# Regrouping the weighted sums of a cross-attention pipeline: four groups a batch, four buffers of exponentials, and new slot tables

## The reference

```
x = layernorm(x + self_attention(x))
x = layernorm(x + cross_attention(x, ctx))   # 16 heads of 8; keys and values are ctx @ Wk + bk, ctx @ Wv + bv
x = layernorm(x + experts(x))                # 8 experts, the best 2 per token, capacity-limited
```

## Time and profile before

| | us |
|---|---|
| median of three runs | 974.03 |
| the profiled execution, device time | 974.64 |
| its span, first to last instruction | 972.5 |
| PE busy | 924.9 (95%) |
| DVE busy | 699.5 (72%) |
| ACT busy | 645.9 (66%) |
| POOL busy | 351.0 (36%) |

### The profile page before, as it was taken

How to read it: one execution, slowest core, us unless ns; L and a number is a source line. 1 busy time by engine, 2 the same in 40 slices (tenths; PEclk the granted TensorE clock), 3 DMA queues, 4 the chain that set the end, 5 groups by cost and what they waited for, 6 DMA issues and landing times.

```text
span 972.5 us, 28783 instructions
## 1 busy us (share of the span) xinstructions
PE 924.9 (95%) x10471; PEld 741.4 (76%) x10471; DVE 699.5 (72%) x1490; ACT 645.9 (66%) x1081; POOL 351.0 (36%) x332
## 2 busy tenths in 40 slices
PE   6777999999999999999999999999999999999995
PEld 4655777777777777777777777777777778999894
DVE  6673777767676677676767767767788857777996
ACT  4654777777777777777777777777776545445554
POOL 6452362222333333222233333332222413112992
PEclk8897999999999999999999999999999999999998
DMA  5538566666655555666666555566665201002321
GB/s 141 121 79 191 120 133 140 143 136 137 137 128 119 119 119 126 141 137 138 136 137 134 119 119 119 120 137 143 137 138 111 69 1 44 23 23 86 128 114 41
DMA packets 43626, 111.44 MB, mean 115 GB/s; under 512 B 15491, under 2 KB 26053, under 8 KB 43461
## 3 DMA queue, kind: packets, MB, share of 16 engines
q1 hardware_dynamic: 43572, 110.77, 50.3%
HBM read 32.23 MB, written 1.89 MB: 35 GB/s over the span
## 4 chain that ended last, share of the span: by engine, by line
PE 84%; ACT 5%; DVE 4%; issue 3%; SPq 2%; POOL 1%; DMA 1%; ACTq 0%; DVEq 0%; POOLq 0%
PE psum L1592 17%; PE psum L1424 16%; PE psum L1652 13%; PE psum L1431 8%; PE psum L1436 8%; PE psum L1656 4%; ACT arena L759 3%; PE psum L1679 2%; PE psum L1692 2%; PE psum L1691 2%; PE psum L1680 2%; PE psum L1681 2%; PE psum L1693 2%; PE psum L1441 1%; SPq L396 1%
## 5 line engine op out<-in xcount | busy, mean ns | idle before, releaser
L946 DVE TENSOR_REDUCE arena<-psum 128x1 f32<-128x500 f32 x672 | 447.8, 674 | 210.1 <-PE psum L1424 206.9
L759 ACT ACTIVATE arena<-psum 125x896 f32<-125x896 f32 x384 | 347.5, 916 | 109.0 <-PE psum L1592 101.7
L1424 PE MATMUL psum<-K_hi,Q_bd 128*128 128x500 f32 x672 | 319.6, 485 | 7.0 <-DVE arena L946 4.1
L547 POOL TENSOR_TENSOR arena<-arena,K_hi 128x500 fp32r<-128x500 f32 x96 | 120.7, 1257 | 403.3 <-ACT K_hi L690 403.3
L1592 PEld LDWEIGHTS psum<-Q_st,K_st 97*125 97x125 f32 x1536 | 221.6, 189 | 42.4 <-ACT arena L759 16.6
L1592 PE MATMUL psum<-Q_st,K_st 97*125 97x224 f32 x1536 | 238.6, 278 | 6.1 <-ACT arena L759 5.6
L1652 PE MATMUL psum<-arena 125*25 125x168 f32 x3072 | 170.5, 311 | 0.2
L1424 PEld LDWEIGHTS psum<-K_hi,Q_bd 128*128 128x128 f32 x672 | 128.6, 192 | 53.3 <-issue 20.8
L813 ACT ACTIVATE K_st<-psum 128x448 fp32r<-128x448 f32 x128 | 69.8, 545 | 79.5 <-PE psum L1681 78.0
L1656 PE MATMUL psum<-arena 125*9 125x56 f32 x3072 | 117.6, 213 | 0.0
L1656 PEld LDWEIGHTS psum<-arena 125*9 125x9 f32 x3072 | 94.1, 91 | 16.6
(11 more groups left out here) (249 smaller groups left out, 983.3 us busy)
## 6 DMA issues: line engine op xcount, KB each, us to landing
K_st<-K_hi SPq DMA_DIRECT2D x256, 187.5 KB, 4.8
K_st<-arena SPq DMA_DIRECT2D x128, 187.5 KB, 3.4
arena<-in_ctx SPq DMA_DIRECT2D x32, 562.5 KB, 6.8
arena<-gate_rows SPq DMA_DIRECT2D x8, 896.0 KB, 4.4
arena<-in_L_ffn_W SPq DMA_DIRECT2D x16, 256.0 KB, 3.2
Q_st<-max_row SPq DMA_DIRECT2D x224, 0.5 KB, 1.7
arena<-OS_all SPq DMA_DIRECT2D x12, 168.0 KB, 4.0
x_rows<-x_all SPq DMA_DIRECT2D x1, 896.0 KB, 6.4
```

Of the source, the lines that this page charges most:

```text
L547: g.tensor_tensor(low.bitcast(F32R), low, K_hi[:, par, n * KB:n * KB + KB].bitcast(F32), ALU.subtract).then_inc(F["keys_low"], 1)
L759: a.activation(P2[c % NP].rearrange("p (n k) -> p n k", n=2), psum[0:CK, 2 + 2 * (c % 2):4 + 2 * (c % 2), 0:HQ // 2], ACT.Exp)\
L946: v.reduce_max(mx[:, n // NB, n % NB:n % NB + 1], bank_of(n)[:, 0:KB], AX.X).then_inc(F["piece_max_taken"], 1)
L1424: mm(bank_of(n)[:, 0:KB], Q_bd[:, par].rearrange("p h q -> p (h q)")[:, 128 * (n // NB):128 * (n // NB) + 128], K_hi[:, par, (n % NB) * KB ...
```

## The change

It changes the order and the groups of the same arithmetic. No matmul, copy or DMA is added to a batch or taken from it.

- The weighted sums of a period stand in four groups of 3, 3, 2 and 4 chunks (slots 3, 6, 9, 11) instead of five of 2, 3, 3, 1 and 3 (slots 2, 5, 8, 10, 11).
- There are four buffers of exponentials instead of three (`NP`), so that an exponential waits for the sums of the chunk four before it.
- Six max pieces of a batch are taken in the period before the one that ends its maxima, instead of nine (`NEXT`). T stands in slot 9 instead of 8, behind V and ahead of O, and two pieces of the next batch come before it instead of one (`BEFORE_TURN`). The array `mx` is held twice.
- The slots of V, K, their copies, the steps on the sums and the scaling move.

```diff
-V_SLOTS = (9, 11, 3)
-K_SLOTS = (5, 6, 8)
-SUM_SLOT, TURN_SLOT = 0, 8
-V_COPIES = (9, 11, 3)
-K_COPIES = (4, 6, 7)
-EARLY_PIECES = {0: (9,), 1: (10,), 2: (11,), 3: (12,), 4: (14,), 6: (18,), 7: (20,), 9: (2,), 10: (4,), 11: (6,)}
-MID_PIECES = {3: (13,), 5: (15, 16), 6: (19,), 8: (0,), 9: (3,), 11: (7,)}
-LATE_PIECES = {5: (17,), 8: (1,), 10: (5,), 11: (8,)}
-OUTPUTS = {2: (0, 1), 5: (2, 3, 4), 8: (5, 6, 7), 10: (8,), 11: (9, 10, 11)}
-NP = 3
+V_SLOTS = (6, 9, 1)
+K_SLOTS = (3, 4, 7)
+COPY_SLOT, SUM_SLOTS, SCALE_SLOT = 0, (0, 1, 2, 2), 3
+ROW_SLOT, TURN_SLOT, KEEP_SLOT = 8, 9, 11
+V_COPIES = (5, 9, 1)
+K_COPIES = (2, 4, 7)
+NEXT, BEFORE_TURN = 6, 2
+EARLY_PIECES = {1: (6, 7), 3: (9, 10), 4: (11, 12), 6: (15,), 7: (19,), 9: (1,), 10: (3,)}
+MID_PIECES = {1: (8,), 6: (16, 17), 11: (4,)}
+LATE_PIECES = {4: (13,), 5: (14,), 6: (18,), 7: (20, 0), 9: (2,), 11: (5,)}
+OUTPUTS = {3: ((0, 0), (0, 1), (0, 2)), 6: ((0, 3), (0, 4), (0, 5)), 9: ((0, 6), (0, 7)), 11: ((0, 8), (0, 9), (0, 10), (0, 11))}
+NP = 4
...
         def bank_of(n):
-            return bank[0 if n == 0 else (n + 1) % 2]
+            return bank[(n + (n >= BEFORE_TURN) + 1 + BEFORE_TURN) % 2]
...
-            row_max(0)
+            row_max(0, 0)
+            for n in range(BEFORE_TURN - 1):
+                piece_max(1, 1, n)
             row_out(0)
...
-                if n == 2:
+                if n == BEFORE_TURN + 1:
                     if turns:
                         pe.wait_ge(F["max_row_ready"], b + PRIME)
...
-            def turn(b):
+            def turn(b, more):
 
                 pe.wait_ge(F["row_max_taken"], b + 1 + PRIME)
+                if more and BEFORE_TURN > 1:
+                    pe.wait_ge(F["piece_max_taken"], (b + 1) * PIECES + BEFORE_TURN - 1 + PRIME)
                 mm(bank[1][0:RG, 0:128], m2x, ident[:], start=True, stop=True).then_inc(F["max_transposed"], 1)
...
-            pieces1(0)
-            turn(0)
-            pieces1(1)
+            pieces1(*range(BEFORE_TURN))
+            turn(0, True)
+            pieces1(BEFORE_TURN)
```

More of the change, by code:

```diff
@@ L75 @@
 PLAIN = 9000.0
[L76 removed]
+ARENA = 19884
 PRIME = 4
@@ L192, in decoder_kernel @@
         inverse = at(128, SLOTS * S // 32)
-        mx = at(128, RG, NB)
+        mx = at(128, 2, RG, NB)
         used[0] = max(used[0], after1)
         K_lo = at(128, NK)
+        yT = [whole[:, used[0] + QC * i:used[0] + QC * i + QC] for i in range(2)]
         ctxT2 = at(DC + 1, 2, NK)
@@ L329, in pieces @@
         def pieces(c, table):
-            return [(2 if n < 9 else 1, n) for n in table.get(c, ())]
+            return [(2 if n < NEXT else 1, n) for n in table.get(c, ())]
         def bank_of(n):
-            return bank[0 if n == 0 else (n + 1) % 2]
+            return bank[(n + (n >= BEFORE_TURN) + 1 + BEFORE_TURN) % 2]
         def has(b, ahead):
@@ L749, in period @@
                 for c in range(NC):
-                    if c == 0 and has(b, -1):
+                    if c == COPY_SLOT and has(b, -1):
                         act.wait_ge(F["outputs_made"], b * NC + PRIME)
@@ L760, in period @@
                          .then_inc(F["weights_ready"], 1)
-                    if c == 9 and has(b, 1):
+                    if c == KEEP_SLOT and has(b, 1):
                         keep_extremes(b + 1)
@@ L939, in _, with piece_max, row_max @@
             dve.wait_ge(consts, 1)
-            def piece_max(b, n):
+            def piece_max(b, par, n):
                 dve.wait_ge(F["max_scores_made"], b * PIECES + n + 1 + PRIME)
[L944 to L948, removed]
+                if n == 0 and (not isinstance(b, int) or b >= 2):
+                    dve.wait_ge(F["row_max_taken"], b - 1 + PRIME)
+                v.reduce_max(mx[:, par, n // NB, n % NB:n % NB + 1], bank_of(n)[:, 0:KB], AX.X).then_inc(F["piece_max_taken"], 1)
+            def row_max(b, par):
                 dve.wait_ge(F["piece_max_taken"], (b + 1) * PIECES + PRIME)
@@ L988, in _, with taken @@
             v.memset(bank[6], 0.0).then_inc(F["bank_cleared"], 1)
[L989 to L992 removed]
+            for n in range(BEFORE_TURN + 2, NEXT):
+                piece_max(1, 1, n)
+            def taken(b, par, c, table):
                 for ahead, n in pieces(c, table):
@@ L995, in taken @@
                         continue
-                    piece_max(b + ahead, n)
+                    piece_max(b + ahead, (par + ahead) % 2, n)
             def period(b, par, half):
                 for c in range(NC):
[L1000 to L1003, removed]
+                    taken(b, par, c, EARLY_PIECES)
+                    taken(b, par, c, MID_PIECES)
+                    if c == ROW_SLOT and has(b, 1):
+                        row_max(b + 1, 1 - par)
                     if c == TURN_SLOT and has(b, 1):
@@ L1023, in period @@
                             v.transpose(R_sb, sums_T).then_inc(F["inverses_turned"], 1)
-                    if c == 4 and has(b, -1):
+                    if c == SCALE_SLOT and has(b, -1):
                         dve.wait_ge(F["inverses_turned"], b + PRIME)
@@ L1534, in _, with bank_free @@
             last.then_inc(w_ps, 1)
-            pieces1(2, 3)
+            pieces1(*range(BEFORE_TURN + 1, BEFORE_TURN + 3))
             pe.wait_ge(F["keys_copied"], 2 * NB + PRIME)
             value_project(1, 0)
-            pieces1(4, 5, 6, 7)
+            pieces1(*range(BEFORE_TURN + 3, NEXT - 1))
             pe.wait_ge(F["values_copied"], NB + 1 + PRIME)
             value_project(1, 1)
-            pieces1(8)
+            pieces1(NEXT - 1)
+            def bank_free(b, kind, n):
+                if isinstance(b, int) and b == B - 2:
+                    pe.wait_ge(F["keys_copied"], B * NB + PRIME)
+                    pe.wait_ge(F["values_copied"], B * NB - 1 + PRIME)
+                    return
+                i = [p[1:] for p in PROJECTIONS].index((kind, n))
+                if isinstance(b, int) and b == 0 and i == 0:
+                    pe.wait_ge(F["values_copied"], NB + 2 + PRIME)
+                _, last, m = PROJECTIONS[i - 1]
+                batch = 1 if last == "values" and m == 2 else 2
+                pe.wait_ge(F[f"{last}_copied"], b * NB + ((batch - (i == 0)) * NB + m + 1) + PRIME)
             def max_scores(b, par, c, table):
@@ L1624, in period @@
                         n = V_SLOTS.index(c)
[L1625 to L1628, removed]
+                        bank_free(b, "values", n)
                         value_project((par + ahead) % 2, n)
@@ L1639, in period @@
                     if c == TURN_SLOT and has(b, 1):
-                        turn(b + 1)
-                    if has(b, 0):
-                        for k in OUTPUTS.get(c, ()):
+                        turn(b + 1, has(b, 2))
+                    for ago, k in OUTPUTS.get(c, ()):
+                        if has(b, -ago):
                             if k == 0:
-                                if isinstance(b, int) and b == 0:
+                                if isinstance(b, int) and b - ago == 0:
                                     pe.wait_ge(F["bank_cleared"], 1 + PRIME)
[L1646 to L1650, removed]
+                                pe.wait_ge(F["values_copied"], (b + (1 - ago)) * NB + PRIME)
+                                if not isinstance(b, int) or b - ago >= 1:
+                                    pe.wait_ge(F["outputs_copied"], b - ago + PRIME)
+                            pe.wait_ge(F["weights_ready"], b * NC + (k + 1 - ago * NC) + PRIME)
+                            weights_, values = P2[k % NP], V2[(par + ago) % 2]
                             for m in range(4):
```

28 lines of the change are left out of this document (13 added, 15 removed).

## The result

The changed kernel takes 1037.64 us (median of four runs, 1034.92 to 1040.92) against 974.5 us for the kernel before beside it: 1.065 of its time, 95% interval 1.061 to 1.069. The forecast was 1000 us, 988 to 1010. The sign was right and the mechanism it named is in the trace; the size was short by 38 us, and the larger part of that belongs to a rival that had been given 3%.

What follows compares the result with a forecast made beforehand. It took PE to bound the kernel before and the row of maxima to bind after the change: 17 + 4.5 + 2.5 + 2 - 0.5 = +25.5 us on 974.0, rounded to 1000 us, range 988 to 1010.

Steps and rivals of the forecast that it cites:

- PE's work: PE in one steady loop period: 22.16 us less 0.33 for a group and 0.44 for a stall, 21.39 us.
- The stall at S of slot 2: PE waiting at S of slot 2 for the exponential of chunk 0: its 0.44 us a period would go.
- the gain of one group: One group of sums fewer on PE in each period: 0.33 us less.
- T's place: T, counted from S of slot 0: starts 16.4 us in, against 13.42 before, with 5.0 us of PE work behind it.
- The row's way: From T through row_out, seven DMA issues and landing: 6.2 us, making a wait of some 1.35 us each period.
- The clock: PE's granted clock in the loop: waits would not lower it, nothing added to the sum.
- rival C: PE's clock in the loop: a wait in every period drops it, 3 to 4.5 us each, 1090 to 1135 us; 3%.
- The start: Up to S of batch 1: later T and row_out(0) and a key copy moved to slot 2, +4.5 us.
- The end: Period of batch 30: DVE's output statistics and a projection stand before row_out and T, +2 us (0 to 3.5).
- A: Loop: the row does not bind, PE's work alone sets the period, some 955 us; 6%.
- B: Loop: the row binds but T comes at 15.8 us, period stays 22.16 us, 974 to 978 us; 3%.
- D: `K_lo` DMAs land over 1.1 us later than reckoned, S of slot 5 waits; at 0.5 a period, 1015 us; 6%.

Runs made afterwards that it cites:

- matmuls in the wait: Changed kernel with its seven DMAs, plus six matmuls of 448 columns ahead of PE's wait for the row in each period: 1014.19 us, 1.042 of before.
- one spare DMA: Changed kernel with one small DMA more ahead of the row's load in the periods of batches 1 to 28: 1062.33 us.
- the kernel with one DMA: Changed kernel with the row of maxima loaded by one DMA a period instead of seven: 957.98 us, 0.984 of before.
- six spare DMAs: Kernel before with six small DMAs issued by SP ahead of the row's load in the periods of batches 1 to 28: 1047.78 us, 1.077 of before.

## Why the prediction was right or wrong

**PE's work.** Right: 21.39 us forecast, 21.31 to 21.45 measured once the row was out of the way. The prices of the groups and the stall, read from the chain, were good to 0.1 us over a period, and K, O and V, T, O without an M between cost about what entries from M cost. The stall at S of slot 2 is gone: in the loop the list of waits has S waiting for no exponential. But what the prediction called the gain of one group is not a gain of the group by itself, as the groups alone gave nothing in the kernel before.

**T's place.** 16.4 us forecast, 16.55 measured; the 0.1 taken off was not there (the sum without it was 16.47). **The row's way** from T: 6.2 to the landing forecast, 0.52 + 5.77 = 6.29 measured; the 0.42 from T to `row_out` was 0.52, and S starts 0.12 to 0.21 after the landing where 0.15 was reckoned. The small terms went the same way, so a plain period takes 23.0 us and not 22.75: 28 x 0.86 = 24 us where the forecast had 16 for as many periods.

**The clock.** This step failed. The prediction put the clock at nothing in its sum and gave rival C 3%: it held that waits of 1.35 us would not lose the clock, because 50 to 80 us in the earlier trace rows had waits up to 1.3 us at a clock of 1.00. The trace has four such waits there, of 1.27, 0.94, 1.05 and 1.03 us. The runs show that waits of such a length lose the clock some of the time, 8 times in 28 periods at 1.2 us and 14 times in 28 at 1.6, and four waits without a fall say little against such a rate. The price of one fall was also taken too high in rival C, 3 to 4.5 us from the fall after 79 us, where the clock was low for four times as long as in the falls of the changed kernel's loop; it is 18.18 - 16.55 = 1.63 us. So the term that was put at nothing is 14 x 1.63 = 23 us in the loop, where rival C had said 90 to 135: rival C was right in kind and wrong in size. The Trainium skill (TensorE: Matmul & The Clock Gate, HAM oscillation) describes a kernel that falls to the low clock in every tile, behind its waits for DMAs. The trace agrees in kind: the falls stand behind waits for a DMA, but behind 14 of 28 and not behind each.

**The start.** S of batch 1 came 5.5 us later, 4.5 forecast. `row_out(0)` and the chain behind it slipped by 2.8 us, not 0.7, as T of batch 0 started at 63.16 and not at 60.39; PE went on at 89.0 against 85.45. That the forecast came so near is in part luck: kernels with the same code up to the wait for that S have it at 105.8 (matmuls in the wait) and 103.9 (one spare DMA) for the changed order, and at 98.5 to 102.7 for the old one, so single traces do not tell 4.5 us from 5.5.

**The end.** The last two periods before batch 31 and the one ahead of them cost 15 us, not the 2 and half of the 5 that were reckoned. The step that failed was to look for what moved ahead of T in the period of batch 30 alone: in all three a gathering step of DVE stood between the last piece and the row maximum, and T came 1.3, 1.3 and 1.8 us later by the kernel with one DMA (S to T 17.84, 17.86 and 18.34 there, 16.5 in the loop). To this come a fall of the clock in each (1.65) and two rows late by 1.2 and 0.7.

**Rivals.** A (the row does not bind) gives 955 us; the changed kernel itself was bound by the row, and the kernel with one DMA, where the row does not bind, takes 958. B falls, as T came at 16.55 us and not at 15.8. D (the low key parts late) is not what happened: from batch 1 on, ACT waited once for these DMAs, 0.85 us in the period of batch 2.

**The sum.** Of the 38 us between 1000 and 1038, the clock's falls are 23 in the loop and 3 more behind it, the row's longer way 8, and the end and the start most of the rest, set off by the tail, which came out 2.3 us shorter and not 0.5. The bounds given for the terms, +12 to +27 and +4 to +12, add up to 990 to 1013 us and not to 988 to 1010; either leaves 1038 outside, as no bound held a term for the clock.

## What to carry to other kernels

Before a step is moved later in an order, add up its way off the engine that does the work (the other engine, every DMA issue one after the other, the landing) and set it against the work that is left behind it; slack that shows in no list of waits is spent first. Where a sum has an engine that was 99% busy come to a wait in every period, price its clock as well, from a stretch with many such waits, not from a few waits elsewhere. A string of small loads whose issues (3.8 us here) add up to more than the transfer (1.7) is a thing to fold into one: here that turned a loss of 6.5% into a gain of 1.6%, and of 2.4% with the start and the end mended.

## What the runs showed of the hardware

- Seven DMAs of 0.5 KB on one queue cost 0.63 us each to issue and land 1.73 us after their issue. One DMA of 3.5 KB, from seven partitions into one, took their place, and S followed T by 4.83 us with no wait, where it had followed by 6.41. The Trainium skill (DMA: Bandwidth & Descriptors, Rules for kernel authors) says to coalesce many small transfers into one large one, as below 64 KB one pays mostly overhead; the trace agrees, 4.83 against 6.41 us.
- A TensorE that was otherwise 99% busy lost the high level of its clock (2.4 GHz) behind waits of 1.2 to 2.2 us, in the traces behind a quarter to a half of them. Behind the ordinary waits of up to 1.0 us it never did; no fall in the loop of any of these traces stands behind less than 0.98 us of idle time. A fall to 1.2 GHz costs 1.63 us in the changed kernel, 1.1 to 1.5 in the kernel before with six spare DMAs. Matmuls of no use, 1.3 us of them in the wait of 1.5, kept it high.
- The price of going into a group of matmuls in narrow column blocks (25 and 9) and out again is 0.33 us by the chain, and the same from a key projection as from a piece: in the changed kernel the first part of the group behind K takes 0.42 us, as in the earlier trace rows.
